# A two-layer transformer on one core: the last routing group rewoven, and five loads moved behind an expert's slots

## The chip, the cores and the metric

The kernel runs on one core of one Trainium2 chip. The metric is the device time of one execution in microseconds. Before the change it was 860.31 us, the median of three runs (859.78 to 861.34).

## What is computed

The input is x, 4 sequences of 1024 tokens with 128 features. Two layers follow each other. Each has a mixing part and a feed-forward part, both behind a layer norm whose scale, shift and gate come from a small product of a per-sequence vector c.

- Layer 0 mixes with a gated linear attention. Its feed-forward part is a mixture of 8 experts with a capacity: every token picks its 2 best experts by its logits, each expert takes its first 640 picks in token order, and a token that comes later gets nothing from that expert.
- Layer 1 mixes with a causal linear attention of 16 heads. Its feed-forward part is a mixture of 16 small experts and 2 shared ones, without a capacity.

The part that matters here is the dispatch of layer 0:

```python
gate_logits = xt @ Wg + bg
top_v, top_i = jax.lax.top_k(gate_logits, TOPK)
expert_label = jax.nn.one_hot(top_i, E).sum(axis=1)
seq = jnp.cumsum(expert_label, axis=0) * expert_label
valid = (seq > 0) & (seq <= capacity)
flat_idx = jnp.where(valid, jnp.arange(E)[None, :] * capacity + (seq - 1), E * capacity)
disp = zeros.at[flat_idx].set(token rows)          # 8 experts x 640 slots
h = silu(disp @ W1) * (disp @ W2); out = h @ W3    # per expert, H = 512
```

The cumulative sum over all tokens is why the last tokens' norm, logits and count have to be over before an expert knows its last slots.

## The kernel before

The 4096 tokens are 32 tiles of 128 (one tile is 128 partitions x 128 features); four tiles are a group, and there are eight groups, 0 to 7 (NGRP = 8, G4 = 4). Each engine has its own function per phase, in which its program order is written out by hand, and the engines meet only at counting semaphores: `wait_ge(S[name], n)` waits until a counter has reached n, `then_inc` raises it. An engine does its instructions in order, so one that waits holds everything behind it.

**The last routing (end of phase 0).** For each group the route of a tile is: VectorE finds the variance (`input_stats`, L837 is its last instruction), a reciprocal root is taken (by GpSimd for early groups, for group 7 by VectorE itself in `last_root`, L942 to L956: nine dependent small steps, three Newton rounds), VectorE multiplies the means (`input_means`, L962), ScalarE writes the normed rows (`input_normed`, L704, one instruction per tile), TensorE transposes them (`input_turned`, L514), ScalarE applies scale and shift (L712), TensorE turns back and takes the logits in one product (`input_rows`, L527), and VectorE adds the gate bias (`input_gated`, L968). `route_labels` (L972 to L995) then finds each token's best two experts (L977, L980), casts them, writes one-hot labels (L986, L990) and two running sums (L992, L994). TensorE counts the queue of each expert with them (`queues_tensor`, L536 to L542), VectorE makes slot numbers of the counts (`route_slots`, L1001 to L1018), and GpSimd sends each tile's rows to the DRAM buffer `disp` by an indirect DMA (`dispatch`, L310), eight per group. For the last group the first four sends carry the lower slot number and the last four the higher one. At the end of VectorE's function the order is: statistics of group 7, gate bias and labels of group 6, root of group 7, means, slots of group 6, then group 7's own labels and slots. TensorE also forms layer 1's modulation gates there: `mod_tensor(1)` (L370), and `gate_tensor(1, 0)` and `gate_tensor(1, 1)` (L382), which ScalarE copies out (`gates_kept`, L629). A barrier of the engines (L104) ends the phase.

**The experts (phase 1).** SyncE's queue carries all plain DMAs. In `experts_sync` it reads expert 0's slots from `disp` (L1139) when all but the last four sends have landed, expert 1's slots (L1121) after the last four, and then layer 1's constants: the output weights twice (L1540, `load_wo`), the cosine table (L1145), the router (L1147) and the down weights (L1148). Then a loop loads, for expert e + 2, the weights (L1111, L1112) and the slots (L1121) as soon as expert e's buffers are free, and the down weights (L1116) after expert e's down product. Weights and slots have two buffers each.

TensorE does eight jobs per expert, four blocks of 128 hidden features times two halves of 320 slots. Each job is two products (gate and up) of three matmuls each (L1244): the fp32 numbers are split into a rounded part and a remainder, and high x high, high x low and low x high are summed. The inputs of expert e + 1 are transposed (`slots_tensor`, L1197; for expert 0 `first_slots_tensor`, L1205) ahead of job 2 of expert e (job 4 for e = 0), and the down product of expert e - 1 (`down_tensor0`, L1279, 20 products that the trace shows as 40) comes right behind that. ScalarE rounds the weights (L1315) and applies silu (L1339), VectorE takes the remainders (L1321), multiplies (L1438), and rounds and subtracts the slots (`first_slots_vector`, L1388 and L1390; L1397 and L1405 for later experts). GpSimd sends each expert's outputs to DRAM, five indirect DMAs (L1183).

The lines that say most about the order:

```python
# experts_sync
self.load_slots(1)
self.load_wo(0)
self.load_wo(1)
...
for e in range(E0 - 2):
    sp.wait_ge(S["e_ws"], NB * (e + 1))
    sp.wait_ge(S["e_tr"], e + 2)
    sp.wait_ge(S["e_to"], e + 1)
    self.load_weights(e + 2)
    self.load_slots(e + 2)
    sp.wait_ge(S["e_down"], e + 1)
    self.load_down(e + 2)
```

## Time and profile before

| what | value |
|---|---|
| median of the runs | 860.31 us (859.78 to 861.34) |
| span of the profiled execution | 860.6 us |
| TensorE matmul busy | 798.8 us, 93% |
| TensorE weight load busy | 695.9 us, 81% |
| VectorE busy | 611.5 us, 71% |
| ScalarE busy | 434.6 us, 50% |
| GpSimd busy | 394.6 us, 46% |
| share of TensorE in the chain that ended last | 72% |
| share of "issue" in it | 13% |
| share of DMA in it | 3% |
| moved by DMA | 49.65 MB, mean 58 GB/s |

One execution was profiled, and its span, 860.6 us, is all that the page gives for its time; it lies 0.3 us above the median of the runs. Busy times are sums over the span. The kernel's stages have different limits, so a mean share says little about the two stretches that the diff touches (about 134 to 197 us from the start of the span); they are read from the chain and the timeline. In the timeline a row is a start in us, a duration in us, the engine, the line of the kernel, the operation, what it writes and reads, how many instructions are merged (x4), and in brackets how long the engine had been idle before and who released it. "remote" is a release for which the trace shows no source.

### The profile page before, as it was taken

To read this page: it belongs to the slowest core of one execution; us is meant where nothing else is said; L and a number is where in the kernel's file an instruction comes from. 1 tells how busy PE (TensorE), PEld (TensorE's weight loads), DVE (VectorE), ACT (ScalarE), POOL (GpSimd) and SP (SyncE) were. 2 spreads that over 40 slices of the span, in tenths; PEclk is the share of its full clock that TensorE was granted. 3 is DMA by queue.
4 is the path that set the end of the run, shared out by engine and by line. 5 is a ranking of instruction groups with operands and counts; after the bars stand their busy time and mean duration, and the time that the engine had idled before them with its cause. 6 is when DMAs were issued, how large, how long until landed. Compare 5 with 4: busy or idle time off the path is not lost.

```text
span 860.6 us, 32362 instructions
## 1 busy us (share of the span) xinstructions
PE 798.8 (93%) x13678; PEld 695.9 (81%) x13678; DVE 611.5 (71%) x1776; ACT 434.6 (50%) x944; POOL 394.6 (46%) x399
## 2 busy tenths in 40 slices
PE   6999984489998799999999999999999999999998
PEld 5777764489997678888889888889888888878887
DVE  7897785357773676676677776787877778757865
ACT  6555533244542665656546566566574645523322
POOL 4357685604544473554645754556643533500000
PEclk9999996599998999999999999999999999999999
DMA  9824000163421200000010000100000000038661
GB/s 294 259 67 161 27 29 13 41 184 102 135 86 45 83 27 4 3 28 4 15 40 4 28 4 3 53 4 4 4 3 3 5 3 3 4 79 148 143 126 39
DMA packets 67904, 49.65 MB, mean 58 GB/s; under 512 B 5322, under 2 KB 62778, under 8 KB 67377
## 3 DMA queue, kind: packets, MB, share of 16 engines
q1 hardware_dynamic: 64288, 42.41, 18.4%
q0 software_dynamic: 3328, 5.16, 1.8%
q8 instruction: 109, 1.79, 0.9%
q14 instruction: 35, 0.28, 0.1%
q10 hardware_dynamic: 144, 0.02, 0.0%
HBM read 33.20 MB, written 16.10 MB: 57 GB/s over the span
## 4 chain that ended last, share of the span: by engine, by line
PE 72%; issue 13%; DVE 6%; DMA 3%; ACT 2%; another core or an unknown queue 1%; SPq 1%; POOL 1%; PEldq 0%; PEld 0%; DVEq 0%; ACTq 0%; POOLq 0%
PE psum L1560 11%; PE psum L1665 7%; PE psum L1716 6%; PE psum L1690 6%; PE psum L1244 6%; PE psum L2349 5%; PE psum L1595 5%; PE psum L1627 5%; PE psum L2367 4%; PE psum L1705 4%; PE psum L1607 3%; PE psum L1578 3%; PE psum L1279 3%; DMA sb_e_x<-disp 1%
## 5 line engine op out<-in xcount | busy, mean ns | idle before, releaser
L1560 PE MATMUL psum<-sb_wkv,sb_a_hs 128*128 128x512 f32 x384 | 122.1, 426 | 1.3 <-ACT sb_a_hs L2036 0.7
L2248 POOL TENSOR_TENSOR sb_a_qr<-sb_h,sb_a_csq 128x512 f32<-128x512 f32 x64 | 81.0, 1288 | 92.0 <-PE psum L1690 88.1
L2248 POOL TENSOR_TENSOR sb_a_qr<-sb_a_qp,sb_a_csq 128x512 f32<-128x512 f32 (+1 forms) x64 | 72.2, 1149 | 94.6 <-PE psum L1690 94.6
L1844 ACT ACTIVATE sb_a_vr<-sb_a_va,sb_consts 128x520 f32<-128x520 f32 x128 | 86.6, 726 | 14.6 <-DVE sb_a_va L2106 14.3
L310 POOL DMA_INDIRECT disp<-sb_h,sb_slot x64 | 67.9, 1062 | 32.2 <-issue 16.9
L1560 PEld LDWEIGHTS psum<-sb_wkv,sb_a_hs 128*128 128x128 f32 x384 | 63.6, 190 | 13.5 <-issue 1.2
L1183 POOL DMA_INDIRECT chosen<-sb_m_h3t,sb_e_row x40 | 39.4, 984 | 69.3 <-ACTq L1357 49.2
L1665 PE MATMUL psum<-sb_a_mid,sb_a_qr 64*64 64x65 f32 x2048 | 70.9, 218 | 0.0
L1244 PE MATMUL psum<-sb_e_xt,sb_e_ws 128*128 128x320 f32 x384 | 65.5, 327 | 5.4 <-issue 4.3
L1690 PE MATMUL psum<-sb_a_vr,sb_a_kb 64*64 64x130 f32 x1920 | 70.1, 272 | 0.0
L1244 PEld LDWEIGHTS psum<-sb_e_xt,sb_e_ws 128*128 128x128 f32 x384 | 59.6, 198 | 9.2 <-issue 5.2
L2127 DVE TENSOR_TENSOR sb_a_mid<-psum,sb_a_state 128x130 f32<-128x130 f32 x112 | 47.3, 423 | 26.0 <-PE psum L1690 26.0
L2106 DVE TENSOR_TENSOR sb_a_va<-psum,sb_rows 128x512 f32<-128x512 f32 x64 | 44.0, 688 | 30.4 <-PE psum L1560 30.4
L1665 PEld LDWEIGHTS psum<-sb_a_mid,sb_a_qr 64*64 64x64 f32 x2048 | 65.2, 134 | 0.1
L1665 PE MATMUL psum<-sb_a_state,sb_a_qr 64*64 64x65 f32 x1792 | 62.7, 218 | 0.0
L2349 PE MATMUL psum<-sb_m_hs,sb_wgus 128*128 128x512 f32 x240 | 60.9, 401 | 0.0
L1813 ACT ACTIVATE sb_a_kt<-psum 128x512 f32<-128x512 f32 x64 | 39.3, 614 | 42.4 <-PE psum L1578 42.4
L1665 PEld LDWEIGHTS psum<-sb_a_state,sb_a_qr 64*64 64x64 f32 x1792 | 57.7, 134 | 0.0
L1690 PEld LDWEIGHTS psum<-sb_a_vr,sb_a_kb 64*64 64x64 f32 x1920 | 57.2, 133 | 0.3 <-issue 0.3
L2424 ACT ACTIVATE sb_m_sg<-psum 128x512 f32<-128x512 f32 x40 | 23.9, 598 | 64.2 <-PE psum L2349 64.2
L1821 ACT ACTIVATE sb_h<-psum,sb_cols 128x512 f32<-128x512 f32 x32 | 22.0, 688 | 59.9 <-PE psum L1595 59.9
L2349 PEld LDWEIGHTS psum<-sb_m_hs,sb_wgus 128*128 128x128 f32 x240 | 43.8, 188 | 9.6
(289 smaller groups left out, 1986.2 us busy)
## 6 DMA issues: line engine op xcount, KB each, us to landing
sb_h<-turned SPq DMA_DIRECT2D x32, 256.0 KB, 5.5
sb_e_w<-in_w SPq DMA_DIRECT2D x24, 256.0 KB
chosen<-sb_empty SPq DMA_DIRECT2D x8, 512.0 KB, 6.1
sb_a_g<-chosen SPq DMA_DIRECT2D x12, 256.0 KB, 3.1
disp<-sb_empty SPq DMA_DIRECT2D x4, 650.0 KB, 9.9
sb_e_x<-disp SPq DMA_DIRECT2D x7, 325.0 KB
sb_a_wo<-in_wo SPq DMA_DIRECT2D x4, 512.0 KB, 4.5
out<-sb_x SPq DMA_DIRECT2D x7, 256.0 KB, 3.9
```

The costliest lines, as they stand in the source:

```text
L310: g.indirect_dma_start(out=self.disp, out_offset=bass.IndirectOffsetOnAxis(ap=self.slot[:, k, n:n + 1], axis=0), in_=self.H2[:, n, :], in_ ...
L1244: ins = pe.matmul(bank[2 * (n % 2) + w][:, 0:HC], self.ews[:, i, wp, w, m * P:(m + 1) * P], self.xeT[:, i, xp, cols], start=(k == 0), stop ...
L1560: ins = pe.matmul(self.values_bank(i) if kv else self.bank[0], hs[:, part, at:at + P], self.Wkv[ws][:, h, w], start=(k == 0), stop=(k == 2))
L1595: ins = pe.matmul(self.bank[2], self.Wq[ws][:, j // PH, (j % PH) * P:(j % PH + 1) * P], hs[:, part, :], start=(k == 0), stop=(k == 2))
L1665: ins = pe.matmul(self.bank[4 + q][c * DH:(c + 1) * DH, j * 65:(j + 1) * 65], Qr[p, k, j, r * DH:(r + 1) * DH], states[r][p, j, k, :], sta ...
L1690: ins = pe.matmul(home[q * DH:(q + 1) * DH, at:at + 130], Kb[t, 2 * j + q, :], Vr[t, 2 * j + q, :, :].rearrange("p k d -> p (k d)"), start ...
L1716: ins = pe.matmul(self.output_home(n), self.oT1[m // PH][n % 2][:, m % PH, :], self.Wog[b % 2][:, m, :], start=(m == 0), stop=(m == HD // ...
L1844: ins = act.activation(self.Vr[i % 2][:, :, k, :], self.Va[i % 3][:], ACT.Copy, scale=self.c[("cos1", "sin1")[k]][:, n:n + 1])
L2106: v.tensor_tensor(self.Va[i % 3][:, :, 0:DH], self.values_bank(i).rearrange("p (h d) -> p h d", d=DH), self.c["bv1"][:, h * 512:(h + 1) * ...
L2127: ins = v.tensor_tensor(part(mid), first, part(state), ALU.add)
L2248: ins = g.tensor_tensor(self.Qr[i % 2][:, k, :, t], qp, rows(self.csQ[:, k, c * P + t.start:(c + 1) * P], PH), ALU.mult)
L2349: ins = pe.matmul(self.hidden_bank(t, w), self.Wgus[wp][:, w, blk * P:(blk + 1) * P], hs[:, xp, :], start=(n == 0), stop=(n == 2))
```

## The change

1. **VectorE, last routing.** The gate bias of group 6 moves ahead of the statistics of group 7. `route_labels` becomes a generator (`label_parts`) that stops eleven times; `last_root` takes it and runs one part ahead of each of its nine dependent steps. The tenth part follows the means, the eleventh follows VectorE's share of the norm, then come the slots of group 6.
2. **The norm of group 7 by two engines.** ScalarE does tiles 0 and 1, VectorE tiles 2 and 3 (`last_normed`); each raises `l0_xn3`, and TensorE waits for both.
3. **TensorE.** The count of group 7 (`queues_tensor(7)`) comes ahead of `gate_tensor(1, 0)`.
4. **SyncE.** Layer 1's five constant loads move from behind expert 1's slots into the loop, behind expert 2's down weights (e == 0).
5. **Experts' first products.** `first_slots_vector` raises `e_xT` for the rounded part and again for the remainder; the three matmuls of a product go high x high, low weights x high slots, high weights x low slots, and the first job waits for the remainder only ahead of its third matmul. The other counts of `e_xT` shift by two.

```diff
     def input_turned(self, c):
-        pe.wait_ge(S["l0_xn3"], c + 1)
+        pe.wait_ge(S["l0_xn3"], c + 1 + (c == NGRP - 1))
...
         self.input_rows(NGRP - 1)
+        self.queues_tensor(NGRP - 1)
         self.gate_tensor(1, 0)
-        self.queues_tensor(NGRP - 1)
         self.gate_tensor(1, 1)
...
     def input_normed(self, c):
-        for i in range(G4):
+        for i in range(G4 if c < NGRP - 1 else G4 // 2):
...
-    def last_root(self):
+    def last_root(self, between):
...
         for n in range(3):
+            next(between)
             v.wait_ge(vs.sem, k)
             k = vs.did(v.tensor_tensor(t, y, y, ALU.mult))
+            next(between)
             v.wait_ge(vs.sem, k)
             k = vs.did(v.tensor_tensor(t, t, h, ALU.mult))
+            next(between)
             v.wait_ge(vs.sem, k)
             ins = v.scalar_tensor_tensor(y, t, 1.5, y, ALU.add, ALU.mult)
...
+    def last_normed(self):
+
+        v, S, c = self.dve, self.S, NGRP - 1
+        v.wait_ge(S["l0_nm3"], NGRP)
+        v.wait_ge(S["l0_xT3"], c)
+        for i in range(G4 // 2, G4):
+            ins = v.tensor_scalar(self.xn3[:, i, :], self.X[:, c * G4 + i, :], self.y3[:, i:i + 1], self.nm3[:, i:i + 1],
+                                  ALU.mult, ALU.add)
+        ins.then_inc(S["l0_xn3"], 1)
...
-    def route_labels(self, c):
+    def label_parts(self, c):
...
         for i in range(G4):
             ins = v.max(self.best[:, i, :], self.LG[:, c * G4 + i, :])
-        v.wait_ge(vs.sem, vs.did(ins))
+            if i == 1:
+                yield
+        n = vs.did(ins)
+        yield
+        v.wait_ge(vs.sem, n)
         for i in range(G4):
             ins = v.max_index(self.which[:, i, :], self.best[:, i, :], self.LG[:, c * G4 + i, :])
-        v.wait_ge(vs.sem, vs.did(ins))
+            if i < G4 - 1:
+                yield
+        n = vs.did(ins)
+        yield
+        v.wait_ge(vs.sem, n)
...
+        self.input_gated(NGRP - 2)
         self.input_stats(NGRP - 1)
-        self.input_gated(NGRP - 2)
-        self.route_labels(NGRP - 2)
-        self.last_root()
+        labels = self.label_parts(NGRP - 2)
+        self.last_root(labels)
         self.input_means(NGRP - 1)
+        next(labels)
+        self.last_normed()
+        next(labels)
         self.route_slots(NGRP - 2)
...
         self.load_slots(1)
-        self.load_wo(0)
-        self.load_wo(1)
-        sp.dma_start(self.csQ[:].rearrange("p k t -> p (k t)"), io["csq"].to_broadcast([P, 2 * T])
-                     ).then_inc(S["dma_l1"], 16)
-        sp.dma_start(self.Wr[:], io["wr"]).then_inc(S["dma_l1"], 16)
-        sp.dma_start(self.Wd[:], io["wd"].rearrange("(m p) d -> p m d", p=P)).then_inc(S["dma_wd"], 16)
         for e in range(E0 - 2):
...
             self.load_down(e + 2)
+            if e == 0:
+                self.load_wo(0)
+                self.load_wo(1)
+                sp.dma_start(self.csQ[:].rearrange("p k t -> p (k t)"), io["csq"].to_broadcast([P, 2 * T])
+                             ).then_inc(S["dma_l1"], 16)
+                sp.dma_start(self.Wr[:], io["wr"]).then_inc(S["dma_l1"], 16)
+                sp.dma_start(self.Wd[:], io["wd"].rearrange("(m p) d -> p m d", p=P)).then_inc(S["dma_wd"], 16)
...
     def slots_tensor(self, e):
-        pe.wait_ge(S["e_xT"], e + 1)
+        pe.wait_ge(S["e_xT"], e + 3)
...
-        three = ((0, 0), (0, 1), (1, 0))
+        three = ((0, 0), (1, 0), (0, 1))
...
-                    pe.wait_ge(S["e_xT"], e + 2 if e else half + 1)
+                    pe.wait_ge(S["e_xT"], e + 4 if e else 3 * half + 1)
...
+                        if j == w == 0 and xp:
+                            pe.wait_ge(S["e_xT"], 2)
...
-            self.slots_rounded = self.vs.did(v.tensor_copy(self.xeT[:, 0, 0, cols], got))
-            v.wait_ge(self.vs.sem, self.slots_rounded)
+            v.tensor_copy(self.xeT[:, 0, 0, cols], got).then_inc(S["e_xT"], 1)
+            v.wait_ge(S["e_xT"], 2 * k + 1)
```

## Rows read from the trace of the kernel before

**Rows 1.** Chain of waits, 120 to 200 us: start us, us, what.
```profile
175.31 8.98 DMA sb_e_x<-disp
```

**Rows 2.** Timeline of SyncE's queue and TensorE, experts 0 to 2.
```profile
169.61 1.15 SPq L1540 DMA_DIRECT2D sb_a_wo<-in_wo  x2
...
173.16 0.43 SPq L1148 DMA_DIRECT2D sb_m_wd<-in_wd  x1
...
184.33 0.77 PE L1197 MATMUL psum<-sb_consts,sb_e_x 128*128 128x128 f32 x5 [1.80 <-DMA sb_e_x<-disp]
...
189.59 0.38 SPq L1116 DMA_DIRECT2D sb_e_w<-in_w  x1
...
191.04 0.43 SPq L1121 DMA_DIRECT2D sb_e_x<-disp  x1
...
196.85 0.71 PE L1197 MATMUL psum<-sb_consts,sb_e_x 128*128 128x128 f32 x5
```

**Rows 3.** Busy time by stretch: engines, clock, DMA share, and GB/s last.
```profile
170.40:181.50 11.10, 10.21 (x56) 9.28 (x56) 8.16 (x22) 4.99 (x13) 0.00 (x0) 0.81 1.09 322
181.50:184.30 2.80, 1.03 (x8) 0.76 (x6) 1.46 (x6) 1.15 (x3) 0.00 (x0) 1.00 0.06 19
```

**Rows 4.** Timeline of the last routing, all engines.
```profile
134.02 1.19 PE L527 MATMUL psum<-sb_consts,sb_h_t 128*128 128x136 f32 x8 [0.87 <-ACT sb_h_t L712]
...
135.61 0.18 DVE L968 TENSOR_TENSOR sb_lg<-psum,sb_rows 128x32 f32<-128x32 f32 x1
...
138.52 0.17 DVE L982 CAST sb_rt_idx<-sb_rt_which 128x8 f32<-128x8 uint32 x1 [1.64 <-remote]
...
139.94 0.19 DVE L990 TENSOR_TENSOR sb_rt_label<-sb_rt_oh 128x32 f32<-128x32 f32 x1 [0.98 <-DVE sb_rt_oh L986]
...
142.83 0.16 DVE L949 TENSOR_TENSOR sb_l_t<-sb_l_y 128x4 f32<-128x4 f32 x1 [2.09 <-remote]
143.53 0.16 DVE L951 TENSOR_TENSOR sb_l_t<-sb_l_t,sb_l_h 128x4 f32<-128x4 f32 x1 [0.54 <-DVE sb_l_t L949]
...
145.80 1.65 ACT L704 ACTIVATE sb_xn<-sb_x,sb_l_nm,sb_l_y 128x128 f32<-128x128 f32 x4 [1.21 <-DVE sb_l_nm L962]
...
147.32 0.97 POOL L310 DMA_INDIRECT disp<-sb_h,sb_slot  x1 [4.95 <-DVE sb_slot L1015]
...
157.91 0.97 POOL L310 DMA_INDIRECT disp<-sb_h,sb_slot  x1 [0.67 <-DVE sb_slot L1018]
...
161.67 0.59 ACT L629 COPY sb_gate<-psum 128x512 f32<-128x512 f32 x1 [7.67 <-remote]
...
163.94 0.91 SPq L1139 DMA_DIRECT2D sb_e_x<-disp  x2
```

**Rows 5.** DMA issues, 140 to 300 us: count, KB each.
```profile
sb_e_w<-in_w SPq DMA_DIRECT2D x18, 256.0 KB
sb_e_x<-disp SPq DMA_DIRECT2D x7, 325.0 KB
```

**Rows 6.** Timeline of TensorE near the last expert.
```profile
272.57 0.70 PE L1244 MATMUL psum<-sb_e_xt,sb_e_ws 128*128 128x320 f32 x3 [3.12 <-issue]
```

**Rows 7.** Busy time by stretches of 1 us; granted clock third from the end.
```profile
184.00:185.00 1.00, 0.67 (x6) 0.67 (x7) 0.00 (x0) 0.06 (x1) 0.00 (x0) 1.00 0.00 0
...
273.00:274.00 1.00, 0.85 (x5) 0.59 (x5) 0.82 (x2) 0.74 (x2) 0.00 (x0) 0.83 0.00 0
...
280.00:281.00 1.00, 1.00 (x9) 1.00 (x8) 0.00 (x0) 0.27 (x1) 0.98 (x2) 0.76 0.10 33
```

**Rows 8.** Line 1244 from 166 to 200 us: durations ns min/median/max.
```profile
L1244 PE MATMUL psum<-sb_e_xt,sb_e_ws x108: 302/309/636, 168.9 to 196.7; 128*128 128x320 f32 x108
```

**Rows 9.** Timeline of expert 0's second half of slots.
```profile
170.22 0.42 DVE L1388 CAST sb_e_xt<-psum 128x256 fp32r<-128x256 f32 x1 [1.45 <-remote]
...
171.16 4.48 PE L1244 MATMUL psum<-sb_e_xt,sb_e_ws 128*128 128x320 f32 x18 [0.35 <-DVE sb_e_xt L1390]
```

**Rows 10.** Line 1183, all sends of the experts: durations ns min/median/max.
```profile
L1183 POOL DMA_INDIRECT chosen<-sb_m_h3t,sb_e_row x40: 967/974/1169, 191.2 to 282.7; - x40
```

More of the change, by code:

```diff
@@ L984, in route_labels @@
         v.tensor_tensor(self.w0[1][:, tiles], self.best[:, :, 1], self.best[:, :, 0], ALU.subtract)
+        yield
         v.wait_ge(vs.sem, n)
@@ L987, in route_labels @@
                                    self.idx[:].unsqueeze(3).to_broadcast([P, 2, G4, E0]), ALU.is_equal))
+        yield
         v.wait_ge(vs.sem, n)
@@ L990, in route_labels @@
         n = vs.did(v.tensor_tensor(label[:, 0, G4:, :], self.oh[:, 0, :, :], self.oh[:, 1, :, :], ALU.add))
+        yield
         v.wait_ge(vs.sem, n)
         n = vs.did(v.tensor_tensor(label[:, 1, G4:, :], label[:, 0, G4:, :], label[:, 0, G4 - 1:2 * G4 - 1, :], ALU.add))
+        yield
         v.wait_ge(vs.sem, n)
@@ L995, in route_labels @@
                         ).then_inc(S["r0_label"], 1)
+        yield
+    def route_labels(self, c):
+        for _ in self.label_parts(c):
+            pass
     def route_slots(self, c):
```

## The prediction

> **What bounds the kernel now.** I read the chain of waits first, then the timeline of the two stretches that the diff touches: the last routing (134 to 164 us) and experts 0 to 2 (164 to 197 us). In the second, TensorE is the bound: it runs with few gaps, and its one clear hole is the wait for expert 2's slots. They are issued at 175.31 and stay on the chain for 8.98 us [rows 1], while TensorE sits idle for 1.80 us until 184.33 [rows 2]. They are late because SyncE issued layer 1's constants from 169.61 to 173.59 ahead of them [rows 2]: the DMA engines moved 322 GB/s for the 11.1 us after 170.4, 3.57 MB in all, and then a thin rest, 19 GB/s for 2.8 us [rows 3]. In the first stretch no engine is full. The order is: VectorE's labels and root, ScalarE's norm at 145.80, TensorE's transposes and rows, labels and slots, GpSimd's sends from 157.91, SyncE's read at 163.94 [rows 4]. GpSimd is nearly a second bound there: from 147.32 it sends expert rows of group 6, one each 1.28 us, eight of them are 10.2 us, so it is free at about 157.6, only 0.3 us ahead of the last group's slots at 157.91 [rows 4].
>
> **Part 1: constants behind expert 2's slots.** What goes: with nothing ahead of them but expert 1's slots, two weight loads and the slots of expert 2 (2 x 256 KB + 325 KB [rows 5], 2.6 us at 322 GB/s, with 1 to 2 us of latency) land near 179.5. TensorE asks for them at 184.33 - 1.80 = 182.53 [rows 2]. The idle 1.80 us goes: **-1.8 us**. What is late next there: nothing, since expert 1's weights and inputs are ready.
>
> What comes: SyncE now issues the constants after expert 2's down weights, that is after TensorE has finished expert 0's down product, 189.59 in the rows of before [rows 2]. All that SyncE issues behind them moves too: expert 3's weights and its slots. Issuing alone costs SyncE 173.59 - 169.61 = 4.0 us [rows 2], so the slots of expert 3 are issued near 195.0 and not at 191.04. They are then queued behind the constants' bytes, as expert 2's were. Bytes ahead of and with them: the 3.57 MB of the old burst, less expert 1's slots (325 KB), plus the down weights (256 KB) [rows 5], plus expert 0's five sends of 128 x 128 floats, 64 KB each, which run at that time: 3.8 MB. At 322 GB/s that is 11.9 us; from 190.6 it ends at 202.5, and with the 2.0 to 2.8 us of thin rest the slots land between 204 and 205. TensorE transposes them at 196.85 [rows 2], with no idle time before, just 7.3 us after the down product. The new hole is 204.4 - 196.85 = **+7.5 us**; both ends of it move with all that is earlier, so the other terms don't change it. The bounds: without the thin rest and the sends' share it is 4.7 us, with all of both 9. ScalarE also waits there, for expert 3's weights in the same queue, but these land about 1 us ahead of the slots, and their casts fit under the next down product, so they add nothing. A later expert doesn't suffer: each has some 12.5 us (184.33 to 196.85 [rows 2]) for 0.8 MB.
>
> The clock: an idle stretch of 3.12 us ahead of 272.57 [rows 6] is followed by a granted clock that falls from 1.00 to 0.50 at about 273.8 (the stretch from 273 to 274 has a mean of 0.83) and returns at about 280.2, from the 2.4 to the 1.2 GHz level; behind the 1.80 us hole it stayed at 1.00 [rows 7]. A hole of 7.5 us will bring it down. At the lower level the same product takes up to 636 ns and not 309 [rows 8], so half of the slow time is lost. Between 273.8 and 280.2 that was 6.4 us with small gaps inside. Behind the new hole stand dense transposes and down products, so I take less, 4 us at the low level: **+2.0 us** (bounds 0 and 3.2).
>
> **Part 2: the last routing.** Four moves act on VectorE's path to the norm.
> - The gating of group 6 now stands ahead of the statistics of group 7. It waits for TensorE's rows, over at 134.02 + 1.19 = 135.2 [rows 4]; the statistics began about 1.2 us before that. +1.2 us.
> - The labels leave the path. From 135.61 VectorE gated and labelled, until 140.6 (three steps of 0.2 us from 139.94) [rows 4]; 1.64 and 0.98 us of it are idle ahead of two instructions [rows 4], the rest is 2.4 us of work. Woven between nine dependent root steps (nine steps and the means took 2.97 us from 142.83 to 145.80, 1.1 us of it idle [rows 4]) they fill the latency of each step and lengthen it little: -2.0 us without the idle times.
> - The norm is split. ScalarE's four took 1.65 us [rows 4]; two take 0.9, beside VectorE's two. -0.7 us, of which one label step ahead of VectorE's part takes 0.2 back.
> - The last label of group 6 now comes just behind VectorE's part of the norm, and TensorE's count for it stands ahead of the last transposes; before it ran under the root. The count is six short products; eight longer ones took 1.19 us at the upper level [rows 4], so six at half the clock are some 1.5 us. +1.4 us.
>
> These four nearly cancel (+0.1).
>
> What is open is the idle time. VectorE stood 1.64, 0.98 and 2.09 us [rows 4] and twice 0.54 us (the first at 143.53 [rows 4]) at waits for its own last result, 5.8 us in all, and no row says why: nothing else ran on it. They lie in 136.9 to 144.3, while GpSimd's sends are in flight. If none recurs, group 6's slots are ready at about 143.0; GpSimd sends from 143.3 for 10.2 us, then four of the last group (5.1 us), and with 1.2 us of landing SyncE reads at 159.8 and not at 163.94: -4.1 us. GpSimd sets it then. If all recur at their old length, the slots of group 6 come near 148.9, later than before (147.32), GpSimd is busy until 159.3, and SyncE reads at 165.3: +1.4 us. The same sends and the same TensorE work stand beside it, so I take a value nearer to the second end than the middle (-1.35) is: **-1.0 us**.
>
> The gates' products behind the count: they free TensorE while it waits anyway, and cost nothing on the path. ScalarE's copy of them ends the phase at 161.67 + 0.6 [rows 4]. They may end 2.1 us later; the cover is the sends. If it were gone (sends early and gates late at once), the phase end, and not the sends, would start the experts: it takes back up to 2 us of the -4.1, none of the -1.0.
>
> **Part 3: first products from the rounded slots alone.** The first job starts 0.6 us earlier, one subtraction. But the second half is rounded at 170.22 after 1.45 us of idle time, and TensorE goes on at 171.16 when that is done [rows 9]. The first job was over 0.35 us before. Value 0; bounds -0.6 and 0.
>
> **A rule of the Trainium skill on the split norm.** All forty sends of the experts took 967 to 1169 ns [rows 10], while VectorE copied and cast beside them, so VectorE's two new scalar operations cost GpSimd nothing in my sum. By the Trainium skill (SBUF — State Buffer, section "SBUF: two separate sides") a fp32 copy in one of VectorE's two-port modes locks GpSimd out of the shared port, and a GpSimd DMA of about 620 ns takes 3100 ns beside it; by that one send would be up to 2.5 us longer, an estimate from that page, and the sum 869.5. The row speaks against it: its longest send is 0.2 us above the shortest.
>
> **Sum.** 860.6 (span; the median of the runs is 0.3 below, which I take off) - 1.8 + 7.5 + 2.0 - 1.0 + 0 = 867.3, less 0.3: **867.0 us**.
>
> **Rivals.**
> 1. *The constants stay hidden (faster).* The transfer decides: if expert 3's slots land within 7.3 us of the down product, no hole comes. 3.8 MB would have to pass at above 500 GB/s, against 322 [rows 3], or the slots would have to overtake what was issued before them, which expert 2's did not (8.98 us [rows 1]). It gives 860.3 - 1.8 - 1.0 = 857.5, and 854.4 with routing at its best. Chance 0.07.
> 2. *A small hole and all idle times gone.* Hole 4.7, no clock loss or little, routing -4.1: 860.3 - 1.8 + 4.7 + 1.0 - 4.1 = 860.1. This is "no change". Chance 0.08.
> 3. *The clock does not fall.* 865.0. The fall after only 3.12 us speaks against it. Chance 0.15.
> 4. *Expert 2's slots are late anyway*, since weights and not constants held them. Then -1.8 is missing: 868.8. Against: the 3.57 MB are mostly constants. Chance 0.07.
> 5. *Routing becomes slower* (+1.4, GpSimd behind later slots) beside the hole: 869.4. Chance 0.18.
> The forecast has the remaining 0.45.
>
> **Range and chances.** A measurement of this kernel tells about 0.2%, 1.7 us, from no change. Rivals 3, 4, 5 and the forecast are slower by more: 0.85. Rival 2 stands for the same: 0.08. Rival 1: faster, 0.07. The bounds of the hole (4.7 to 9) with routing -2 to +1.4 and the clock 1 to 3 give 862 to 872; leaving out the thin ends, 862.0 to 871.0.
>
> **What would show it.** Right: TensorE's idle time ahead of expert 2's transposes gone; 6 to 9 us of idle ahead of expert 3's, released by the slots' DMA; a granted clock of 0.5 for some 4 us behind it; expert 2's slots landing in about 4 us, expert 3's in about 9. SyncE's first read of slots between 160 and 165.5, GpSimd without a gap between groups 6 and 7. Wrong: no idle time ahead of expert 3's transposes, a DMA rate much above 322 GB/s, or an unbroken clock of 1.0 behind the hole.

## The result, and the profile after

The changed kernel takes 869.89 us (median of 7 runs, 865.38 to 873.72); the kernel before, beside it, 861.36 us (7 runs, 859.78 to 864.36). The ratio is 1.0092, with a 95% interval of 1.0065 to 1.0118: 7.9 us slower, 5.6 to 10.2 (the medians lie 8.5 apart). The time of a run is 1.3 to 1.4 us longer than its span. So the profile of before, with its span of 860.6 us, shows an execution slightly slower than the median, and the profiled execution of the changed kernel (866.51 us, span 865.1) is among its fastest: the two profiles show only 4.5 us of the difference. The ratios leave out runs more than 1.5% above the fastest of their kernel; below, that is one run of free_after, 870.27 us.

Page of the changed kernel, busy times:

```profile
span 865.1 us, 32363 instructions
PE 797.7 (92%) x13678; PEld 694.4 (80%) x13678; DVE 605.3 (70%) x1778; ACT 433.2 (50%) x942; POOL 393.5 (45%) x399
```

Lines of the file have moved by some 13 to 36 (L1197 of before is L1231, L1244 is L1280, L1121 is L1154, L1111 to L1116 are L1144 to L1149).

**The last routing** of the changed kernel, timeline of all engines (start, us, what; in brackets the idle time before it and what ended it):

```profile
134.31 2.18 PE L527 MATMUL psum<-sb_consts,sb_h_t 128*128 128x136 f32 x8 [0.87 <-issue]
...
136.53 0.19 DVE L981 TENSOR_TENSOR sb_lg<-psum,sb_rows 128x32 f32<-128x32 f32 x1 [1.38 <-PE psum L527]
...
140.98 0.16 DVE L953 TENSOR_TENSOR sb_l_t<-sb_l_t,sb_l_h 128x4 f32<-128x4 f32 x1 [1.10 <-DVE sb_l_t L950]
...
142.40 0.18 DVE L956 SCALAR_TENSOR_TENSOR sb_l_y<-sb_l_t,sb_l_y 128x4 f32<-128x4 f32 x1 [1.11 <-issue]
...
143.83 0.17 DVE L1003 CAST sb_rt_idx<-sb_rt_which 128x8 f32<-128x8 uint32 x1 [1.25 <-DVE sb_l_y L956]
...
145.98 0.88 ACT L704 ACTIVATE sb_xn<-sb_x,sb_l_nm,sb_l_y 128x128 f32<-128x128 f32 x2 [3.96 <-DVE sb_l_nm L975]
145.98 0.62 DVE L967 TENSOR_SCALAR sb_xn<-sb_x,sb_l_y,sb_l_nm 128x128 f32<-128x128 f32 x2
146.52 0.18 DVE L1019 TENSOR_TENSOR sb_rt_label<-sb_rt_label 128x32 f32<-128x32 f32 x1
...
146.76 0.64 PE L536 MATMUL psum<-sb_rt_label,sb_consts 128*128 128x32 f32 x2 [7.91 <-DVE sb_rt_label L1019]
...
148.29 0.19 DVE L1031 COPY sb_rt_cum<-psum 128x32 f32<-128x32 f32 x1 [1.58 <-PE psum L542]
...
149.93 0.97 POOL L310 DMA_INDIRECT disp<-sb_h,sb_slot  x1 [6.57 <-DVE sb_slot L1045]
...
161.36 0.58 ACT L629 COPY sb_gate<-psum 128x512 f32<-128x512 f32 x1 [2.28 <-remote]
...
166.17 0.91 SPq L1172 DMA_DIRECT2D sb_e_x<-disp  x2
```

Against [rows 4]: VectorE's labels and root, now interleaved, have again three idle times of over 1 us at waits for its own last result, and a fourth of 1.38 us, for TensorE's rows. The norm begins at 145.98, no earlier than before (145.80). Behind it come VectorE's share of the norm, the last label, the count, and only then the slots of group 6 (the copy at 148.29). GpSimd's sends start at 149.93 and not at 147.32, and SyncE reads 2.2 us later. (How much of the 2.2 us is the change, and how much this pair of executions, is taken up in the part on the prediction.)

**The experts**, timeline of SyncE's queue, TensorE and ScalarE:

```profile
175.26 0.71 PE L1231 MATMUL psum<-sb_consts,sb_e_x 128*128 128x128 f32 x5
...
182.16 0.71 PE L1231 MATMUL psum<-sb_consts,sb_e_x 128*128 128x128 f32 x5
...
187.36 0.38 SPq L1149 DMA_DIRECT2D sb_e_w<-in_w  x1
187.78 1.14 SPq L1576 DMA_DIRECT2D sb_a_wo<-in_wo  x2
...
193.07 0.63 SPq L1154 DMA_DIRECT2D sb_e_x<-disp  x1
...
195.39 0.70 PE L1280 MATMUL psum<-sb_e_xt,sb_e_ws 128*128 128x320 f32 x3 [1.03 <-DVE sb_e_hs L1474]
...
200.09 0.71 ACT L1351 CAST sb_e_ws<-sb_e_w 128x256 fp32r<-128x256 f32 x2 [3.39 <-DMA sb_e_w<-in_w]
201.02 1.33 PE L1231 MATMUL psum<-sb_consts,sb_e_x 128*128 128x128 f32 x5 [4.92 <-DMA sb_e_x<-disp]
202.14 6.99 PE L1315 MATMUL psum<-sb_e_w,sb_e_hs 128*128 128x128 f32 x40
...
216.87 0.77 PE L1231 MATMUL psum<-sb_consts,sb_e_x 128*128 128x128 f32 x5 [0.30 <-issue]
```

Its chain of waits at that place:

```profile
193.07 7.91 DMA sb_e_x<-disp
```

And its busy time by stretch, one of the routing and two of the experts (start and end, us; PE, PEld, DVE, ACT, POOL; granted clock; DMA share; GB/s):

```profile
135.00:136.00 1.00, 1.00 (x6) 1.00 (x6) 0.15 (x1) 0.00 (x0) 0.70 (x1) 0.50 0.09 23
...
187.40:200.00 12.60, 7.66 (x48) 6.72 (x46) 5.96 (x15) 5.68 (x14) 4.86 (x5) 0.87 0.95 306
...
203.00:204.00 1.00, 1.00 (x6) 1.00 (x6) 0.97 (x3) 0.00 (x0) 0.00 (x0) 0.50 0.00 0
```

The 1.80 us of idle time ahead of expert 2 [rows 2] are gone. In their place TensorE waits 4.92 us for expert 3's slots, issued behind the constants at 193.07 and 7.91 us on their way. The granted clock is 0.50, the 1.2 GHz level, from about 196.9 to 207.0. Five transposes take 1.33 us there and 0.71 at the full clock, the 40 products of the down step 6.99 us.

Where the 4.5 us of the profiled execution arise, from the starts of the transposes in both timelines (those of before that are not in [rows 2, 4] read from its timeline in the same way):

Each value is one execution.

| stretch | before | after | difference |
|---|---|---|---|
| start to SyncE's read of the slots | 163.94 | 166.17 | +2.2 |
| to expert 1's transposes | 11.54 | 9.09 | -2.4 |
| to expert 2's | 8.85 | 6.90 | -2.0 |
| to expert 3's | 12.52 | 18.86 | +6.3 |
| to expert 4's | 12.44 | 15.85 | +3.4 |
| to the last part of the last expert | 50.22 | 50.12 | -0.1 |
| to layer 1's first transposes | 23.61 | 20.61 | -3.0 |
| layer 1 | 577.5 | 577.5 | 0 |

The -3.0 stem from the last expert, where no edit is: its idle time was 2.53 us and not 3.12 [rows 6], and the clock stayed up behind it.

```profile
279.48 2.11 PE L1280 MATMUL psum<-sb_e_xt,sb_e_ws 128*128 128x320 f32 x12 [2.53 <-ACT sb_e_sg L1375]
282.25 2.94 PE L1336 MATMUL psum<-sb_e_w,sb_h 128*128 128x128 f32 x24 [0.66 <-DVE sb_h L1474]
```

The same 24 products took 4.74 us in the profile of before. This is chance and not the change: from expert 7's transposes to layer 1 it took 35.8 us before and 32.8 us here, and between 33.0 and 36.9 us in the twelve kernels below, none of which touches that place.

### The profile page after: what moved, and what is told of

Its sections match the earlier page's. It is cut to its first block, busy times and chain, and to the rows that moved or that the text cites. A ratio compares the mean times of both kernels' runs of the same rounds, so it can differ in the third digit from the quotient of the medians.

```text
span 865.1 us, 32363 instructions
## 1 busy us (share of the span) xinstructions
PE 797.7 (92%) x13678; PEld 694.4 (80%) x13678; DVE 605.3 (70%) x1778; ACT 433.2 (50%) x942; POOL 393.5 (45%) x399
## 4 chain that ended last, share of the span: by engine, by line
PE 72%; issue 14%; DVE 6%; DMA 3%; ACT 2%; SPq 2%; POOL 1%; another core or an unknown queue 0%; DVEq 0%; ACTq 0%; POOLq 0%
PE psum L1596 11%; PE psum L1701 7%; PE psum L1726 6%; PE psum L1752 6%; PE psum L1280 5%; PE psum L2385 5%; PE psum L1631 5%; PE psum L1663 5%; PE psum L2403 4%; PE psum L1741 3%; PE psum L1315 3%; PE psum L1643 3%; PE psum L1614 3%; DMA sb_e_x<-disp 1%; PE psum L1336 1%
## 5 line engine op out<-in xcount | busy, mean ns | idle before, releaser
L1596 PE MATMUL psum<-sb_wkv,sb_a_hs 128*128 128x512 f32 x384 | 122.3, 426 | 1.7 <-ACT sb_a_hs L2072 0.7
L1596 PEld LDWEIGHTS psum<-sb_wkv,sb_a_hs 128*128 128x128 f32 x384 | 63.6, 190 | 13.8 <-issue 1.2
L1280 PE MATMUL psum<-sb_e_xt,sb_e_ws 128*128 128x320 f32 x384 | 63.1, 319 | 4.7 <-ACT sb_e_sg L1375 2.5
L1280 PEld LDWEIGHTS psum<-sb_e_xt,sb_e_ws 128*128 128x128 f32 x384 | 57.4, 191 | 8.4 <-DVE sb_e_hs L1474 3.0
```

What stands on the lines that cost most here:

```text
L1280: ins = pe.matmul(bank[2 * (n % 2) + w][:, 0:HC], self.ews[:, i, wp, w, m * P:(m + 1) * P], self.xeT[:, i, xp, cols], start=(k == 0), stop ...
L1596: ins = pe.matmul(self.values_bank(i) if kv else self.bank[0], hs[:, part, at:at + P], self.Wkv[ws][:, h, w], start=(k == 0), stop=(k == 2))
```

## The experiments

The theory is that of the prediction: the constants only move their hole to expert 3, with the clock on top, and the new routing doesn't gain. The rivals are that the routing carries the loss, that another place for the constants has no hole at all, and, for VectorE's idle times, that TensorE's work causes them and not GpSimd's sends.

Each ratio compares a kernel with runs of the kernel before in the same sessions: 863.51 us (31 runs) for the four kernels beside each other, 860.94 us (13 runs) for first_only, sends_held, mod_later and filled, 865.21 us (17 runs) for filled2, the pads and free_first. The 31 runs lie between 859.65 and 869.09, so a single profile can be off by several us from another execution of the same kernel.

### Which part costs what: four kernels beside each other

**consts_only**: the kernel before with the constants' loads alone moved.

```diff
-        self.load_wo(0)
...
             sp.wait_ge(S["e_down"], e + 1)
             self.load_down(e + 2)
+            if e == 0:
+                self.load_wo(0)
...
```

> The kernel before with one edit: layer 1's five constant loads stand behind expert 2's down weights. Theory A (the loads open a hole of about 5 us ahead of expert 3's slots, the clock falls behind it and costs 3 us, and expert 2's 1.8 us hole goes): 6 us slower than before, 3 to 8. Theory B (the slowdown comes from the last routing): within 1.7 us of before or 1.8 us faster.

Measured: 870.1 us (864.44 to 874.92, 10 runs), ratio 1.0048 (1.0012 to 1.0084). Timeline of TensorE:

```profile
203.29 1.33 PE L1198 MATMUL psum<-sb_consts,sb_e_x 128*128 128x128 f32 x5 [5.98 <-DMA sb_e_x<-disp]
204.41 6.21 PE L1280 MATMUL psum<-sb_e_w,sb_e_hs 128*128 128x128 f32 x40
```

No idle time ahead of expert 2's transposes (184.41), 5.98 ahead of expert 3's, 18.88 us later, the same distance as in the changed kernel (18.86). This part alone makes the kernel slower, by 4.1 us (1.0 to 7.3); the medians differ by 6.6 us.

**no_consts**: the changed kernel with the loads back at their old place.

```diff
         self.load_slots(1)
+        self.load_wo(0)
...
             self.load_down(e + 2)
-            if e == 0:
-                self.load_wo(0)
...
```

> The changed kernel with the five constant loads put back behind expert 1's slots; routing and first products stay changed. Theory A: within 2.5 us of the kernel before: SyncE's first read of slots is 2 us later, and the first products give that back. Theory B: as slow as the changed kernel, 5 us or more above before.

Measured: 866.03 us (863.59 to 868.49, 10 runs), ratio 1.0031 (1.0008 to 1.0054). SyncE reads at 166.08. Timeline of TensorE:

```profile
185.45 0.79 PE L1230 MATMUL psum<-sb_consts,sb_e_x 128*128 128x128 f32 x5 [3.33 <-DMA sb_e_x<-disp]
186.06 6.26 PE L1314 MATMUL psum<-sb_e_w,sb_e_hs 128*128 128x128 f32 x40
```

Routing and first products together are slower by 2.7 us (0.7 to 4.7). The old hole is longer here, 3.33 us and not 1.80, and it now brings the clock down too: the down product takes 6.26 us, against 4.63 at the full clock. The two parts add up: 4.1 + 2.7 = 6.8 us of the 7.9, each with an interval of 2 to 3 us to either side. The routing alone was not run.

**free_before** and **free_after**: in the kernel before and in the changed one, the constants stand behind expert 2's slots, but ahead of the wait for expert 0's down product and not behind it. SyncE waits there anyway.

```diff
+            if e == 0:
+                self.load_wo(0)
...
             sp.wait_ge(S["e_down"], e + 1)
             self.load_down(e + 2)
```

> The kernel before with the five constant loads between expert 2's slots and the wait for expert 0's down product, so that no later slots stand behind them. Theory A: expert 2's hole of 1.8 us goes and none comes ahead of expert 3's slots: 1.8 us faster, 1 to 3. Theory B: no difference. Rival to A: the transfers still run when expert 3's weights are issued, and a small hole of 1 to 2 us stays: no difference.

> The changed kernel with the constant loads between expert 2's slots and the wait for expert 0's down product. Theory A: the hole of 4.9 us and the 3 us at the low clock go; 2 us faster than the kernel before, between 0 and 4. Theory B: still slower than the kernel before by 3 us or more.

Measured: free_before 862.06 us (860.19 to 865.11, 10 runs), ratio 0.9989 (0.9967 to 1.0011); free_after 863.93 us (857.22 to 870.27, 10 runs), ratio 0.9998 (0.9965 to 1.0031). Expert 2's transposes start at 182.62 and 181.80, expert 3's at 195.08 and 194.29, all without idle time ahead. So neither hole need be: it is the wait for the down product, standing ahead of the constants, that costs. By the ratios free_after is some 8 us faster than the changed kernel. But against the kernel before, taking both holes away gains nothing that this measurement shows. Layer 1 begins 3.9 us earlier in free_before (279.22, against 283.12), and then takes 583.0 us and not 577.5. Layer 1's length differs by up to 5.5 us between kernels whose layer 1 is the same, each profiled once, and differences of this size hide the gain. Whether they go with the kernel or with the execution, one profile each can't tell.

### The first products

**first_only**: the kernel before with the first products' edit alone (item 5 of the change; part 3 of the prediction).

```diff
-        pe.wait_ge(S["e_xT"], e + 1)
+        pe.wait_ge(S["e_xT"], e + 3)
...
-        three = ((0, 0), (0, 1), (1, 0))
+        three = ((0, 0), (1, 0), (0, 1))
...
-                    pe.wait_ge(S["e_xT"], e + 2 if e else half + 1)
+                    pe.wait_ge(S["e_xT"], e + 4 if e else 3 * half + 1)
...
+                        if j == w == 0 and xp:
+                            pe.wait_ge(S["e_xT"], 2)
...
-            self.slots_rounded = self.vs.did(v.tensor_copy(self.xeT[:, 0, 0, cols], got))
-            v.wait_ge(self.vs.sem, self.slots_rounded)
+            v.tensor_copy(self.xeT[:, 0, 0, cols], got).then_inc(S["e_xT"], 1)
+            v.wait_ge(S["e_xT"], 2 * k + 1)
```

> The kernel before with the first products' edit alone (the rounded slots are signalled apart from the remainder, order high x high, low weights x high slots, high x low). My prediction gave it 0, bounds -0.6 and 0. In the changed kernel the first expert's products began 2.1 us later than before and were over 0.2 us earlier; if the edit does that, TensorE reaches expert 1's transposes 1.5 to 2 us earlier and the time falls by as much, less what the wait for expert 2's slots (unchanged here) takes: then the end does not move. If VectorE's idle time of 1.45 us there is chance: 0 to 0.6 us.

Measured: 861.24 us (858.15 to 862.87, 10 runs), ratio 1.0011 (0.9991 to 1.0031). Timeline of TensorE:

```profile
166.13 1.98 PE L1246 MATMUL psum<-sb_e_xt,sb_e_ws 128*128 128x320 f32 x6 [0.27 <-issue]
...
169.06 5.17 PE L1246 MATMUL psum<-sb_e_xt,sb_e_ws 128*128 128x320 f32 x18 [0.95 <-DVE sb_e_xt L1392]
```

The first job starts early, and TensorE waits the longer for the second half, 0.95 us and not 0.35 [rows 9]. From SyncE's read to expert 1's transposes: 12.10 us here; 11.54, 12.97 and 11.18 in kernels with the old order (before, consts_only, free_before); 9.09, 8.98 and 10.47 in those with the new routing as well (changed kernel, no_consts, free_after). So the new order alone gives nothing; with the new routing beside it 0.7 to 4 us are gained there. It need not be the order that gains them even then: sends_held, below, has the old order and the old routing but later sends, and takes 9.76 us. VectorE's idle time of 1.45 us ahead of the second half [rows 9] is 1.50 us here, and is missing in the changed kernel and in sends_held. What removes it wasn't tried.

### VectorE's idle times

**sends_held**: in the kernel before, GpSimd's sends of group 5 wait for the last root. (One run.)

```diff
                 g.wait_ge(S["l0_H2"], c + 1)
+                if c == NGRP - 3:
+                    g.wait_ge(S["l0_root3"], NGRP)
```

> The kernel before, but GpSimd's sends of group 5 wait until VectorE's last root is done. Nothing is left out. It tells whether the sends in flight cause VectorE's idle times at its own results (5.8 us from 136.9 to 144.3). If they do: labels and root of 4.2 us of work run without them, ScalarE's last norm begins near 140. If not: the same idle times, last norm near 145.8. The whole will be slower, since GpSimd sends later.

Measured: 865.43 us. Timeline of all engines:

```profile
138.30 0.19 DVE L992 TENSOR_TENSOR sb_rt_label<-sb_rt_oh 128x32 f32<-128x32 f32 x1
...
138.86 0.17 ACT L617 COPY sb_mt<-psum 128x8 f32<-128x8 f32 x1 [1.54 <-PE psum L372]
...
141.09 1.65 ACT L706 ACTIVATE sb_xn<-sb_x,sb_l_nm,sb_l_y 128x128 f32<-128x128 f32 x4 [1.91 <-DVE sb_l_nm L964]
141.65 0.97 POOL L312 DMA_INDIRECT disp<-sb_h,sb_slot  x1 [8.72 <-DVE sb_l_y L955]
142.79 1.11 PE L516 MATMUL psum<-sb_consts,sb_xn 128*128 128x128 f32 x4 [2.31 <-ACT sb_xn L706]
...
150.18 1.14 PE L384 MATMUL psum<-sb_consts,sb_gateb 128*128 128x128 f32 x8
...
158.57 0.59 ACT L631 COPY sb_gate<-psum 128x512 f32<-128x512 f32 x1 [9.28 <-remote]
```

VectorE runs labels and root without one idle time, and the last transposes are 4.7 us earlier than before (142.79, against 147.50). ScalarE's copy ahead of the root waits 1.54 us, and 7.87 us in the profile of before. The sends come later themselves, SyncE reads at 168.13, and the whole doesn't gain. So the idle times need the sends: that is shown, by one execution. But sends beside a chain of small steps are not enough. In the kernel before, group 7's labels run beside the sends of group 6 (from 147.32 on) from 151.71 to 154.63 with one idle time of 0.27 us:

```profile
154.44 0.19 DVE L994 TENSOR_TENSOR sb_rt_label<-sb_rt_label 128x32 f32<-128x32 f32 x1 [0.27 <-DVE sb_rt_label L992]
```

In sends_held itself they run from 146.99 to 149.43, beside sends from 141.65 on, with none. Later in the same burst of sends it is ScalarE that is late: its copy of the last gates starts at 158.57, and the product that it waits for, the last rows of TensorE above, was over at 151.3; in the kernel before the same copy is 3.6 us late (161.67 [rows 4], its product over at 158.0). What decides when an engine is late, and which, stays open.

**mod_later**: in the kernel before, the short product for the gates' factor stands behind group 6's count on TensorE. (One run.)

```diff
-        self.mod_tensor(1)
         self.queues_tensor(NGRP - 2)
+        self.mod_tensor(1)
```

> The kernel before, with TensorE's product for layer 1's modulation behind the count of group 6 and not ahead of it. VectorE's idle times begin right behind that product's start. If the product causes them: VectorE's labels and root run through, last norm near 140 to 141. If not: idle times as before, last norm near 145.8.

Measured: 861.65 us. Timeline of TensorE:

```profile
139.89 0.64 PE L536 MATMUL psum<-sb_rt_label,sb_consts 128*128 128x32 f32 x2 [4.54 <-DVE sb_rt_label L994]
...
146.53 1.11 PE L514 MATMUL psum<-sb_consts,sb_xn 128*128 128x128 f32 x4 [2.63 <-ACT sb_xn L704]
```

From TensorE's rows (133.18) to the last transposes it takes 13.35 us, against 13.5 before and 8.5 with sends_held. VectorE's idle times are spread otherwise, but come to 5.0 us again. The order of these two products on TensorE is not the cause.

### The clock behind the new hole

**filled**: the changed kernel, with 32 transposes of the identity ahead of expert 3's, into a bank that the next product overwrites.

```diff
         pe.wait_ge(S["e_xT"], e + 3)
+        if e == 3:
+            for _ in range(32):
+                pe.transpose(bank[6][:, 0:P], self.c["ident"], self.c["ident"])
```

> The changed kernel with 32 transposes of the identity on TensorE ahead of the wait for expert 3's slots; they write a bank that the real transposes overwrite and fill some 4.5 us of the hole at the upper clock. If the clock's fall behind the hole costs what the trace suggests (down product 6.99 us and not 4.63, transposes 1.33 and not 0.71): granted clock 1.00 behind the hole, 3 us faster than the changed kernel. If the fall is set by something else than TensorE's idle time: the clock falls all the same, and the time is that of the changed kernel or up to 0.5 us more.

Measured: 900.26 us (898.76 to 902.61, 4 runs), ratio 1.0459 (1.0414 to 1.0505). I put them behind the wait for the slots' DMA and not ahead of it, so they stood on the path and filled nothing:

```profile
199.16 6.25 PE L1231 MATMUL psum<-sb_consts 128*128 128x128 f32 x32 [7.11 <-DMA sb_e_x<-disp]
```

But 6 us don't make 31. Layer 1 begins at 292.12 and takes 608.3 us and not 577.5: a surprise, which the pads below follow up.

**filled2**: six products of 512 columns ahead of the wait for the slots' DMA.

```diff
-        pe.wait_ge(S[f"dma_e_x{i}"], 16 * (e // 2 + 1))
         pe.wait_ge(S["e_xT"], e + 3)
+        if e == 3:
+            for _ in range(6):
+                pe.matmul(bank[6].rearrange("p (a d) -> p a d", a=4), self.c["ident"], rows(self.c["ident"], 4), start=True, stop=True)
+        pe.wait_ge(S[f"dma_e_x{i}"], 16 * (e // 2 + 1))
```

> The changed kernel with six products of 512 columns on TensorE ahead of the wait for expert 3's slots (their result is overwritten). They take some 5 us at the upper clock and stand inside the hole. The run named filled put its transposes behind the wait for the DMA, so it did not test this. If TensorE's idle time brings the clock down: clock 1.00 behind the hole, transposes 0.71 and down product 4.6 us (1.33 and 6.99 in the changed kernel), and layer 1 begins 2 to 3.5 us earlier against the first transposes of expert 0. If something else does: down product 6 to 7 us all the same. The whole time may be spoilt by a second effect, see pad32, and is not the measure here.

Measured: 879.62 us (878.2 to 882.64, 3 runs), ratio 1.0167 (1.0139 to 1.0195). Timeline of TensorE:

```profile
196.09 5.31 PE L1230 MATMUL psum<-sb_consts 128*128 128x512 f32 x12
201.86 0.77 PE L1234 MATMUL psum<-sb_consts,sb_e_x 128*128 128x128 f32 x5 [0.46 <-DMA sb_e_x<-disp]
202.46 4.63 PE L1318 MATMUL psum<-sb_e_w,sb_e_hs 128*128 128x128 f32 x40
...
214.45 0.74 PE L1234 MATMUL psum<-sb_consts,sb_e_x 128*128 128x128 f32 x5
```

The fillers end 0.46 us ahead of the slots. With them the granted clock stayed at 1.00, the 2.4 GHz level; the down product takes 4.63 us and not 6.99, and expert 4's transposes come 2.4 us earlier than in the changed kernel (214.45, against 216.87), though expert 3's come 0.8 us later. So the clock costs 2.4 to 3.3 us of the change. Layer 1 begins at 284.93, 2.7 us earlier than in the changed kernel, and takes 592.0 us: this loss again, and larger than the gain.

### What more instructions do to layer 1

**pad32** and **pad16**: the kernel before, with 32 or 16 transposes of the identity ahead of TensorE's wait for expert 0's slots.

```diff
         pe, S = self.pe, self.S
+        for _ in range(32):
+            pe.transpose(self.bank[6][:, 0:P], self.c["ident"], self.c["ident"])
         for k, part in enumerate(self.FIRST):
```

> The kernel before with 32 transposes of the identity on TensorE ahead of expert 0's wait for its slots, where TensorE has been idle for 8.7 us. In the run named filled, 32 more transposes came with a layer 1 that took 608 us and not 578, with 24 us of idle time of TensorE that nothing releases. If the place of the later code in the instruction stream does that: layer 1 takes 600 us or more here too, and the whole is about 30 us slower, though nothing on the path has more work. If it came from the later start of layer 1 or from the missing hole: no difference from the kernel before, at most 1 us.

> The same with 16 transposes. If the place of the code matters, layer 1 takes another time again, anywhere between 578 and 610 us; if not, as before.

Measured: pad32 893.18 us (889.29 to 893.82, 3 runs), ratio 1.0305 (1.0276 to 1.0334); pad16 879.1 us (877.31 to 882.07, 3 runs), ratio 1.0159 (1.0131 to 1.0188). Timeline of TensorE, pad32:

```profile
165.99 5.11 PE L1203 MATMUL psum<-sb_consts 128*128 128x128 f32 x32 [7.29 <-PEq L104]
```

Waits of TensorE (us in all, times, longest), pad32, then pad16, then the kernel before:

```profile
PE psum L1707 <- issue: 22.6, 20, 1.6
```

```profile
PE psum L1707 <- issue: 16.0, 15, 1.5
```

```profile
PE psum L1705 <- issue: 2.1, 3, 1.2
```

Layer 1 begins at 284.40 and 284.71, only 1.3 and 1.6 us later than before, and takes 608.1 and 596.1 us, against 577.5. Its own work is the same to the instruction. TensorE stands still at one line of it, 20 and 15 times for 1.1 us on average, with nothing that the profile shows to wait for; in the kernel before and in the others without pads or fillers it did so 3 times. These waits are 22.6 of the 30.6 us and 16.0 of the 18.6. A later start of layer 1 is not the cause: in the changed kernel it begins 4.5 us later than before and takes 577.5 us. Only the number of instructions that TensorE has ahead of layer 1 differs, 32 or 16 products with their weight loads. How that number leads to the idle times stays open.

### The two cheap edits together

**free_first**: the kernel before with the constants placed as in free_before and the first products as in first_only; the routing stays as it was.

> The kernel before with two edits: the constant loads between expert 2's slots and the wait for expert 0's down product, and the first products from the rounded slots. The first takes expert 2's hole of 1.8 us away, and then nothing hides what the second gives (0 to 2 us). Expected 2 us faster than before, between 0 and 4. If the two only shift TensorE's idle time into layer 1: no difference.

Measured: 863.29 us (858.38 to 866.23, 12 runs), against 865.21 for the kernel before in the same session; ratio 0.997 (0.9947 to 0.9993). Expert 2's transposes start at 184.24, expert 3's at 196.73, both without idle time ahead. By its runs it is faster than the kernel before by 2.6 us (0.6 to 4.6), and so than the changed one too. Against the kernel before this is weak: the interval only just leaves out no change, its two edits alone gave -0.9 us (-2.8 to 0.9) and +0.9 us (-0.8 to 2.7), and its own profile, of the slowest of its 12 runs, doesn't show where a gain would come from.

## Why the prediction was right, and where its sizes were off

The forecast was 867.0 us, within 862.0 to 871.0, and slower; it came out as 869.89. The mechanism was the one forecast: the constants brought a hole ahead of expert 3's slots, the clock fell behind it, and the new routing gained nothing to set against them. The terms, one by one:

- **Expert 2's hole, -1.8: right.** It measured -2.0 in the profile. free_before shows that it doesn't reach the end by itself: -0.9 us (-2.8 to 0.9).
- **Expert 3's hole, +7.5: mis-sized, measured +6.3** (18.86 - 12.52), within the bounds of 4.7 to 9. 4.92 of them are the wait for the slots, 1.03 an idle time of TensorE just before it. From the end of the down product to the slots' landing (201.0) it took 13.6 us, and the sum had 14.8 (189.59 to 204.4). The rate was as assumed, 306 GB/s over the whole stretch against 322 [rows 3]; the thin rest was some 1 us, from 200 on, and not 2.0 to 2.8. The step that ScalarE's wait for expert 3's weights adds nothing held: ScalarE did wait 3.39 us for them, but its cast begins at 200.09, 0.9 us ahead of the slots' landing. The 1.03 us were released by VectorE's product (L1474), not by those weights.
- **The clock, +2.0 (0 to 3.2): mis-sized, measured +3.4** from expert 3's to expert 4's transposes, and 2.4 to 3.3 by filled2. The granted clock was at 0.50 for 10 us, of which TensorE worked 6.0 (201.02 to 207.0) and not 4; half of that, 3.0 us, is lost, and 0.30 us are idle time ahead of 216.87. That the products behind the hole are dense did not shorten it.
- **The routing, -1.0 (-4.1 to +1.4): this step failed, measured +2.2** in the two profiles. I had leaned on VectorE's idle time not coming back in part. At waits for its own last result it was 5.8 us before, and it is 4.6 in the changed kernel (0.19, 1.10, 1.11, 1.25, 0.39 and 0.54 in its timeline from 139.5 to 145.4): most of it recurred. So it did in every profile with the sends in their place: 5.1 to 6.0 us in seven kernels with the old routing (before, consts_only, free_before, first_only, free_first, pad16, pad32), 4.1 to 5.1 us in five with the new one (changed kernel, no_consts, free_after, filled, filled2). The 1.2 us less were used up at once, because the gating now stands ahead of the statistics and waited 1.38 us for TensorE's rows. From the means to the copy of the count took 0.08 us before and 2.5 us now (145.78 to 148.29), of which I had counted 1.4 + 0.2: VectorE's own half of the norm, 0.5 us ahead of the last label, and the way to TensorE and back were missing. From there GpSimd's sends of 1.28 us each carry it, as foretold: from the first send of group 6 to SyncE's read it takes 16.2 to 16.6 us with either routing. The case "all recur" (+1.4) should have been the forecast. Its working is not whole, either: the four moves come to +0.1, and how the slots of group 6 then get from 147.32 to 148.9 isn't said.
- **How much of the +2.2 is the change.** From TensorE's rows (L527, 134.02 before and 134.31 after) to SyncE's read it took 29.7 to 31.0 us in the seven kernels with the old routing, 30.5 in the mean, and 31.6 to 32.6 us in the five with the new one, 31.9 in the mean. The profile of before, with 29.9, is a fast one at this place. So the new routing costs some 1.4 us, the upper bound of the term, and the rest of the 2.2 is this pair of executions.
- **The split of the norm, -0.7:** ScalarE's part took 0.88 us as counted, but TensorE was then busy with the count, so the last transposes came at 148.06 and not at 147.50. The page's rule that VectorE locks GpSimd out (the Trainium skill, SBUF — State Buffer, section "SBUF: two separate sides") was not put to a test there: GpSimd was idle from 143.4 to 149.93, so no send ran beside the two new operations. The forty sends of [rows 10] were not all the evidence that the trace of before had. Among the sends to `disp` some took 1.5 us and not 0.97, those beside VectorE's products of two operands in SBUF (at 61.5, 91.5, 106.5 and 122.3 us, for example): half a microsecond longer, where the page's figures for a copy would give 2.5.

```profile
L310 POOL DMA_INDIRECT disp<-sb_h,sb_slot x64: 967/974/1518, 57.8 to 167.1; - x64
```

- **The gates' products, 0: right.** ScalarE's copy of the last gates ended at 161.9, before at 162.3 [rows 4], both ahead of SyncE's read.
- **The first products, 0 (-0.6 to 0): right alone** (first_only: +0.9 us, -0.8 to 2.7). Beside the rest the stretch that they stand in was 2.4 us shorter in the profile, outside the bounds. The sum took its terms as independent, and they are not. In no_consts TensorE also reached expert 1's transposes after 8.98 us, but then waited 3.33 us for expert 2's slots, which the constants held up: only with the constants moved does such a gain get through.

By the parts of the change the sum is 2.2 - 2.4 - 2.0 + 6.3 + 3.4 = 7.5 us (and 860.3 + 7.5 = 867.8), where the forecast had 6.7. That the two are so near is in part luck: the routing was 3.2 us worse than forecast and the first experts' stretch 2.4 us better, the clock 1.4 us worse and the hole 1.2 us better. The profiled execution gave back 3.0 at the last expert by chance. The measured 7.9 us (5.6 to 10.2) agree with the parts.

Of the rivals, the fifth (routing slower, 869.4) came nearest, though with other sizes: the routing cost as much or more than it had, the hole less. Rival 1, constants hidden, is what free_before shows to be possible; the transfer itself fits under experts 1 and 2 when SyncE need not wait first. Rival 3 fell: the clock went down. Of the signs, two were outside what was named: TensorE's idle time ahead of expert 3's transposes was 4.92 us and not 6 to 9, and SyncE's first read came at 166.17 and not by 165.5.

## What to carry to other kernels

A load that has to be moved is worth following to the next wait of its queue: behind the wait for the down product the constants were as late for expert 3 as they had been for expert 2, and a few lines earlier, ahead of a wait in which the queue stood idle anyway, they opened no hole at all. A short idle stretch of TensorE has a second price, the products at half the clock behind it, and it may be as large as half of the first. Idle time without a visible cause in a chain of small steps should be taken to recur where what runs beside it stays, and moving work off such a chain gains nothing while another engine, here GpSimd with its sends, sets the end and now starts later.

## What the runs showed that was not expected

GpSimd's sends in flight can make other engines late at their waits. With the sends of group 5 held back, VectorE's 5.8 us of idle time in labels and root went to nothing, and a copy of ScalarE waited 1.54 us and not 7.87. It is no steady price of a send: the same steps ran beside sends almost without idle time elsewhere (0.27 us and none, above), and in sends_held another copy of ScalarE was 7 us late. Which part of a send does this, its issue or its transfer, and why only at times, no run here tells.

Instructions of TensorE that cost little where they stand can cost 14 to 31 us much later (by the whole times, the pads cost 13.8 and 26.4 us). 16 transposes under a wait made layer 1, 120 us behind them, 18.6 us longer, 32 made it 30.6 us longer, 32 at another place (filled) 30.8, and six products of 512 columns (filled2, 12 records) 14.5. The same line of layer 1 took the idle times each time. Small differences between kernels are therefore to be read per stretch: layer 1 took between 577.5 and 583.0 us in the kernels without pads or fillers, though no edit touched it. And a stretch of one profile is to be read beside the same stretch of others: the +2.2 us of the routing shrank to some 1.4 that way.
